# A state-space layer and a gated feed-forward: scans joined over both halves of a column, with states and decays in SBUF

## What is computed

```python
def first(x):                       # applied to layernorm(x); the result is added to x
    x, z = split(x_in @ W_in)       # 256 and 256 columns
    proj = x @ W_x                  # 256 of delta, 16 of B, 16 of C
    delta = softplus(proj[..., :256] @ W_dt + b_dt)
    dA  = exp(delta[..., None] * -exp(A_log))          # (b, l, d, n)
    dBx = (delta * x)[..., None] * B[:, :, None, :]
    def step(h, inp):
        dA_t, dBx_t, C_t = inp
        h = dA_t * h + dBx_t                            # a state for each d and n
        return h, einsum('bdn,bn->bd', h, C_t)
    y = scan(step, 0, ...) + x * D_param
    y = y * silu(z) @ W_out
    return layernorm(y + x_in) * ln_g + ln_b

def second(x):                      # applied to layernorm(x); the result is added to x
    x_prev = x shifted by one token
    r = sigmoid((mu_r*x + (1-mu_r)*x_prev) @ W_r.T)
    k = (mu_k*x + (1-mu_k)*x_prev) @ W_k.T
    return r * (square(relu(k)) @ W_v.T)
```

## Time and profile before

| | |
|---|---|
| median of 3 runs | 942.68 us (942.14 to 942.72) |
| the profiled execution | 944.42 us, its span 942.6 us |
| instructions | 15838 |
| mean granted TensorE clock | 0.973 |
| DVE | 900.9 us busy, 96% |
| POOL | 889.1 us, 94% |
| PE | 864.2 us, 92%; weight loads 688.7 us |
| ACT | 847.9 us, 90% |
| DMA | 163.60 MB, mean 174 GB/s |

### The profile page before, as it was taken

The page is one execution under the profiler, slowest core; times in us unless marked ns, Lnnn a source line. Parts: engine busy times, 40 slices in busy tenths (PEclk is TensorE's granted clock), DMA queues, the critical chain, the costliest instruction groups (busy, mean ns, idle before and its releaser), DMA issues.

```text
span 942.6 us, 15838 instructions
## 1 busy us (share of the span) xinstructions
PE 864.2 (92%) x5024; PEld 688.7 (73%) x5024; DVE 900.9 (96%) x985; ACT 847.9 (90%) x2064; POOL 889.1 (94%) x399
## 2 busy tenths in 40 slices
PE   8757679999999899989999899998999999999998
PEld 5545567877878587787868678786778768778876
DVE  4899989999999999999999999999999999999896
ACT  5886988989999999998999999999999999978875
POOL 4999999999999999999999989999999999999970
PEclk9987898999999999999999999999999999999999
DMA  7445435462534644455463644446354354446231
GB/s 222 156 177 204 175 138 204 179 235 104 210 157 161 239 164 172 183 178 166 174 248 147 224 148 160 179 179 248 125 210 179 143 198 179 157 160 223 91 101 45
DMA packets 49938, 163.60 MB, mean 174 GB/s; under 512 B 5248, under 2 KB 33152, under 8 KB 33600
## 3 DMA queue, kind: packets, MB, share of 16 engines
q1 hardware_dynamic: 48528, 161.27, 46.2%
q0 software_dynamic: 512, 1.31, 0.5%
q10 hardware_dynamic: 816, 0.02, 0.1%
HBM read 153.15 MB, written 9.44 MB: 172 GB/s over the span
## 4 chain that ended last, share of the span: by engine, by line
PE 46%; ACT 28%; DVE 15%; issue 9%; DMA 1%; POOL 0%; POOLq 0%; DVEq 0%; SPq 0%; ACTq 0%
PE w_ps L1326 10%; ACT da_ps L654 10%; PE y_ps L1317 9%; PE w_ps L1350 6%; DVE da_ps L1033 5%; PE w_ps L1359 4%; PE w_ps L1362 4%; DVE hg L1049 3%; DVE hg L1033 3%; PE w_ps L1465 3%; DVE hg L1040 2%; PE w_ps L1368 2%; ACT xn_tok L591 2%; ACT h_tok L591 2%; ACT zs L715 2%
## 5 line engine op out<-in xcount | busy, mean ns | idle before, releaser
L542 POOL TENSOR_TENSOR dbx<-u,b_ring 128x1024 f32<-128x1024 f32 x255 | 599.4, 2380 | 4.7 <-DVE hg L1033 4.6
L654 ACT ACTIVATE da_ps<-delta,a_neg 128x512 f32<-128x512 f32 x512 | 340.0, 684 | 23.9 <-DVE hg L1040 7.3
L555 POOL TENSOR_TENSOR hg<-hg,c_ring 128x1024 f32<-128x1024 f32 x122 | 290.4, 2381 | 8.5 <-ACT carry L660 6.7
L1317 PE MATMUL y_ps<-ident,hg 128*128 128x128 f32 x2048 | 264.3, 279 | 9.2 <-POOL hg L555 9.0
L1317 PEld LDWEIGHTS y_ps<-ident,hg 128*128 128x128 f32 x2048 | 241.7, 145 | 35.9 <-issue 17.8
L1033 DVE TENSOR_TENSOR_SCAN da_ps<-da_ps,carry,dbx 128x512 f32<-128x512 f32 x203 | 249.8, 1271 | 4.3 <-ACT da_ps L654 4.1
L1033 DVE TENSOR_TENSOR_SCAN hg<-da_ps,carry,dbx 128x512 f32<-128x512 f32 x181 | 220.3, 1263 | 1.4 <-ACT carry L660 1.2
L1040 DVE TENSOR_TENSOR hg<-da_ps,c_ring 128x1024 f32<-128x1024 f32 x68 | 82.3, 1210 | 0.2
L1049 DVE TENSOR_TENSOR hg<-da_ps,c_ring 128x512 f32<-128x512 f32 x130 | 82.3, 673 | 0.0
L1033 DVE TENSOR_TENSOR_SCAN da_ps<-da_ps,dbx 128x512 f32<-128x512 f32 x64 | 75.8, 1213 | 3.3 <-ACT da_ps L654 2.8
L1326 PE MATMUL w_ps<-xnT_ring,w_in 128*128 128x512 f32 x120 | 61.4, 636 | 16.0 <-ACT xT L696 14.1
(11 more groups left out here) (212 smaller groups left out, 1333.0 us busy)
## 6 DMA issues: line engine op xcount, KB each, us to landing
c_ring<-bc_rows_dram SPq DMA_DIRECT2D x64, 1024.0 KB, 4.7
b_ring<-bc_rows_dram SPq DMA_DIRECT2D x63, 1024.0 KB, 6.7
xres<-in_L_attn_x_in_dram SPq DMA_DIRECT2D x16, 512.0 KB, 4.8
x_tok<-in_L_attn_x_in_dram SPq DMA_DIRECT2D x15, 512.0 KB, 5.9
out_dram<-r_out SPq DMA_DIRECT2D x14, 512.0 KB, 3.2
bc_rows_dram<-bc_rows SPq DMA_DIRECT2D x64, 16.0 KB, 5.4
w_in<-in_L_attn_W_in_dram SPq DMA_DIRECT2D x2, 256.0 KB, 4.3
x_tok<-in_L_attn_x_in_dram SPq DMA_DIRECT2D x2, 256.0 KB, 4.6
```

Source lines behind the costliest of these rows:

```text
L542: pool.tensor_tensor(dbx[:, n % X_RING, :, :], u[:, ip, :, :], b.to_broadcast([P, KH, LC]), ALU.mult).then_inc(s["dbx_done"], 1)
L555: pool.tensor_tensor(part, part, c_of(n).to_broadcast([P, KH, LC]), ALU.mult).then_inc(s["g_pool"], 1)
L654: act.activation(da_of(n, h), delta[:, ip, h, :], ACT.Exp, scale=a_neg[:, h, n:n + 1]).then_inc(s["da_ready"], 1)
L1317: last = pe.matmul(y_tok[:, b, h * P:(h + 1) * P], hg[:, n % H_RING, h, b * P:(b + 1) * P], ident[:, :], is_transpose=True, start=n == 0 a ...
```

## The change

**One scan for a column.** `decay`, `dbx`, `u` and `hg` get rows of 515 cells (`EXT`) for each half: two lead cells, 512 tokens (`TOK`), and one cell behind. The two halves lie behind one another, so one scan of 1030 elements does both. The first cell of each half has decay 0, which ends the half before; the second has decay 1. The lead cells of `u` are 1, 0 in the first half and 0, 1 in the second; the lead cells of a B row are the two carries of that column. So POOL's product of `u` and B puts each half's carry into its lead cells, and the scan begins from there without a scalar operand. The cell behind has decay 1 and input 0: it keeps the last state where the multiplication by C, which covers only the tokens, doesn't reach it.

**Carries.** ACT copies the carries of four columns at once out of `hg` (`keep_carries`, place `KEEP_AT`) and feeds them, four columns at once, into the lead cells of the B rows (`feed_carries`, place `FEED_AT`). POOL's product waits for the feed (`carry_fed`); DVE's first scan of a group waits until the carries that its slots held are saved.

**Places in memory.** The decays are in SBUF, `decay`, a ring of three columns; the states of every column go to `hg` in SBUF, and DVE's multiplication by C works there, always in one instruction for both halves. The three PSUM banks of `da_ps` become work banks: `W_BANKS` is 6. `spare` is gone, `xn_tok` and `h_tok` serve in its place.

**Columns and places.** DVE multiplies 10 columns of a step by C in place of 8 or 9, POOL 6 in place of 7 or 8. The turn tables and `BANK` are new; of them two lines stand in the diff.

```diff
-SPLITS = [[0, 2, 5, 6, 8, 11, 12, 14], [0, 2, 3, 5, 6, 8, 11, 12, 14]]
+SPLITS = [[0, 2, 3, 5, 8, 9, 11, 12, 13, 15], [0, 2, 3, 5, 6, 9, 11, 12, 13, 15]]
-                sum1=15, sq1=16, x0=18, tanh=19, ln_exp=20, rs1=22, x1=22, sq20=22, sq21=23, rs2=23, k1=24, square=24,
+                sum1=16, sq1=17, x0=18, tanh=20, ln_exp=22, rs1=20, x1=25, sq20=23, sq21=23, rs2=23, k1=24, square=25,
-W_BANKS = 3
+W_BANKS = 6
+KEEP_AT, FEED_AT = 10, 10
-DA_BANKS = 3
+A_RING = 3
+LEAD = KH
+EXT = LEAD + LC + 1
+TOK = slice(LEAD, LEAD + LC)
...
-        u = sb("u", P, 2, KH, LC)
+        u = sb("u", P, 2, KH, EXT)
+        decay = sb("decay", P, A_RING, KH, EXT)
-        b_ring = sb("b_ring", P, BG, GN, LC)
+        b_ring = sb("b_ring", P, BG, GN, EXT)
-        dbx = sb("dbx", P, X_RING, KH, LC)
-        hg = sb("hg", P, H_RING, KH, LC)
+        dbx = sb("dbx", P, X_RING, KH, EXT)
+        hg = sb("hg", P, H_RING, KH, EXT)
...
-                sp.dma_start(b_ring[:, g % BG, :, :],
+                sp.dma_start(b_ring[:, g % BG, :, TOK],
                              bc_dram[i, GN * g:GN * g + GN, :].partition_broadcast(P)).then_inc(b_loaded[g], 16)
...
+                need(pool, s["carry_fed"], GROUPS * i + n // GN + 1)
...
-                pool.tensor_tensor(dbx[:, n % X_RING, :, :], u[:, ip, :, :], b.to_broadcast([P, KH, LC]),
+                pool.tensor_tensor(dbx[:, n % X_RING, :, :], u[:, ip, :, :], b.to_broadcast([P, KH, EXT]),
                                    ALU.mult).then_inc(s["dbx_done"], 1)
...
-                act.activation(da_of(n, h), delta[:, ip, h, :], ACT.Exp,
-                               scale=a_neg[:, h, n:n + 1]).then_inc(s["da_ready"], 1)
+                need(act, s["scan_done"], NS * i + n - A_RING + 1)
+                act.activation(decay_of(i, n)[:, h, TOK], delta[:, ip, h, :], ACT.Exp,
+                               scale=a_neg[:, h, n:n + 1]).then_inc(s["da_ready"], 1)
...
+            def keep_carries(t, g):
+                need(act, s["scan_done"], NS * t + GN * (g + 1))
+                slot = GN * g % H_RING
+                act.activation(carry[:, GN * g:GN * (g + 1), :], hg[:, slot:slot + GN, :, EXT - 1],
+                               ACT.Copy).then_inc(s["carry_saved"], 1)
+
+            def feed_carries(t, g):
+                need(act, s["dbx_done"], NS * t + GN * (g - BG + 1))
...
+                src = no_carry[:, :, :] if first else carry[:, GN * g:GN * (g + 1), :]
+                act.activation(b_ring[:, g % BG, :, 0:LEAD], src, ACT.Copy).then_inc(s["carry_fed"], 1)
...
-                for h in range(KH):
-                    in_bank = n in split_of(t) or t == LAST and n == NS - 1 and h == 1
-                    out = da_of(n, h) if in_bank else hg[:, n % H_RING, h, :]
-                    dve.tensor_tensor_scan(out, da_of(n, h), dbx[:, n % X_RING, h, :],
-                                           0.0 if first else carry[:, n, h:h + 1], ALU.mult, ALU.add).then_inc(s["scan_done"], 1)
+                if n % GN == 0:
+                    before = t if n >= H_RING else t - 1
+                    if before >= 0 and not ends(before):
+                        dve.wait_ge(s["carry_saved"], kept_groups(before) + (n - H_RING) // GN % GROUPS + 1)
...
+                dve.tensor_tensor_scan(flat(hg[:, slot, :, :]), flat(decay_of(t, n)), flat(dbx[:, at, :, :]),
+                                       0.0, ALU.mult, ALU.add).then_inc(s["scan_done"], 1)
...
-                dve.tensor_tensor(hg[:, n % H_RING, :, :], da_both(n), c_of(n).to_broadcast([P, KH, LC]),
+                part = hg[:, n % H_RING, :, TOK]
+                dve.tensor_tensor(part, part, c_of(n).to_broadcast([P, KH, LC]),
                                   ALU.mult).then_inc(s["g_vec"], 1)
```

More of the change, by code:

```diff
@@ L76, in ends @@
     return (i + 1) % CPB == 0
[L79 to L87, removed]
 def need(eng, sem, count):
@@ L193, in mamba_rwkv_layer @@
         y_tok = y_ps[:, :, :].rearrange("p a (b d) -> p (a b) d", d=D)
-        da_ps = ps("da_ps", P, DA_BANKS, LC)
         work = [ps(f"w{b}_ps", P, LC) for b in range(W_BANKS)]
-        START_BANKS = ([y_ps[:, m, :] for m in range(KH)] + [work[W_BANKS - 1][:, :]]
-                       + [da_ps[:, m, :] for m in range(DA_BANKS)])
+        START_BANKS = ([y_ps[:, m, :] for m in range(KH)] + [w[:, :] for w in work[HEAD_BANK:]])
         names = """w_in_loaded w_x_loaded w_dt_loaded w_bc_loaded w_z_loaded w_z_halved a_loaded w_loaded mu_loaded w_r_in w_kv_in ffn_turned ffn_set ident0 ident_done flags_done
@@ L323, in by_half @@
             return b[:, :].rearrange("p (k n) -> p k n", k=KH)
-        GT_LAST = K_LAST = [da_ps[:, v, :] for v in range(2)]
-        WO_LAST = R_LAST = [da_ps[:, 2, :], work[0][:, :]]
+        GT_LAST = K_LAST = [work[W_BANKS - 3 + v][:, :] for v in range(2)]
+        WO_LAST = R_LAST = [work[W_BANKS - 1][:, :], work[0][:, :]]
         HT_LAST = [y_ps[:, v, :] for v in range(2)]
@@ new lines, in scans @@
+                if t == n == 0:
+                    dve.wait_ge(s["flags_done"], FLAGS)
+                need(dve, s["y_added"], NS * t + n - H_RING + 1)
+                if n % GN == 0:
+                    before = t if n >= H_RING else t - 1
+                    if before >= 0 and not ends(before):
+                        dve.wait_ge(s["carry_saved"], kept_groups(before) + (n - H_RING) // GN % GROUPS + 1)
+                if t == n == 0 or t == LAST and n == NS - 1:
+                    for h in range(KH):
+                        if t == 0:
+                            dve.wait_ge(s["dbx_done" if h else "dbx_begun"], 1)
+                        else:
+                            need(dve, s["dbx_done"], NS * t + n + 1)
+                        need(dve, s["da_ready"], KH * (NS * t + n) + h + 1)
+                        dve.tensor_tensor_scan(hg[:, slot, h, :], decay_of(t, n)[:, h, :], dbx[:, at, h, :],
+                                               0.0, ALU.mult, ALU.add).then_inc(s["scan_done" if h else "half_scanned"], 1)
+                    return
@@ L1553, in late_v @@
                     by_token(V_LATE[v], v, kact, w_vT).then_inc(late_v_done, 1)
-                pe.wait_ge(s["scan_done"], KH * (NS * NT - 1))
-                need(pe, s["g_vec"], splits(LAST, NS - 1))
+                for b in range(W_BANKS - 3, W_BANKS):
+                    pe.wait_ge(work_read[b], sum(len(units_of(v, b)) for v in range(NT)))
                 residual(0)
```

226 lines of the change are left out of this document (98 added, 128 removed).

## The result

The changed kernel takes 1500.93 us (median of 4 runs, 1500.21 to 1503.3), the kernel before 942.7 us beside it: a ratio of 1.593, 95% interval 1.590 to 1.596. The profiled execution has a span of 1499.2 us.

A forecast was written before the change was run, and what follows sets the result against it. DVE and POOL, both full side by side, were taken to bound the kernel; taking turns, DVE's 563 + 176 and POOL's 591 + 228 add to 1558 us, with 52 at the ends 1610 us; range 1310 to 1735.

The forecast's parts named there:

- The step that decided: DVE scans and C products reading two SBUF tensors take turns with POOL products by the instruction, so times add; chance 0.78.
- The one collision from before: Kernel before, from 20.69 us: a DVE SBUF-to-SBUF `xn_tok<-x_tok` stood still 952 ns until POOL's first product ended.
- the lower end of this case: Turns by the instruction with each fixed part hidden in the wait: elements alone add to 1513 us, span 1565.
- rival B: Turns by the element: half of a scan's time stays open to POOL, 274 us less, 1336 us; chance 0.06.
- the term for POOL in the sum: 255 B products and 99 C products at full spacing, 591 + 228 us, added to DVE's time; elements only, 573 + 221.
- DVE's other groups: Six DVE groups with a PSUM operand, 125 us, can run beside POOL; up to 60 us extra only in the upper bound.
- DVE's own parts: Without turns: 254 scans of 2289 ns and 156 C products of 1216 ns, by spacing 563 us with half scans, and 176.
- ACT, the table loads, the feeds and the B rows: ACT's 27 us loss hides behind the turns; feed waits and B rows loaded as four pieces are taken at nothing.
- TensorE's granted clock: It can fall towards the lower 1.2 GHz level; even doubled work of 106 us makes a step only 8 us longer.
- Rival A: No turns between DVE and POOL: about 928 us if DVE sets the end, about 950 if ACT does; chance 0.14.
- rival C: The change doesn't do what it says, for lack of new B rows or banks: about 1000 to 1060 us; chance 0.02.
- The signs that I named: Step near 98 us, scan or `dbx` maxima about 4.6 us, PSUM groups at 0.67, DVE and POOL near 90%, ACT 55%.

The follow-up runs named there:

- experiment 1: Small kernel without the layer, DVE and POOL instructions alone and paired: ten SBUF scans took 22.06 us alone, 40.94 beside ten POOL products.
- experiment 3: Kernel before with DVE operands read from constant SBUF: products by C 1191.64 us, scans 1485.28, both 1646.82.
- experiment 4: Changed kernel with the tables of before: 1509.83 us; also scan decays from PSUM after step 0: 1121.20; also C products' states from PSUM: 1006.85.
- experiment 2: Second small kernel varying sizes and kinds of instruction: ten DVE scans took 31.24 us beside POOL products of 512, 29.19 beside POOL scalings, 22.06 alone.
- both_sbuf: Kernel before with both the scans' decay and the C products' state operand read from a constant SBUF tensor: 1646.82 us, ratio 1.745.

## Why the prediction was right, and where its size was off

The step that decided held: DVE and POOL take turns when DVE reads two SBUF tensors, by the instruction. The one collision from before, 952 ns, was of the same kind, with one SBUF tensor as in the copy of experiment 1. By the Trainium skill's page "SBUF — State Buffer", section "Who interferes with whom", the second input of DVE comes through the interface that GpSimd reads by; experiments 1, 3 and 4 agree, scans included, and its sentence that a GpSimd instruction that only writes is no obstacle to two inputs agrees with the scan beside memsets (22.06 us both ways). The prediction left out a condition of that section, by which one SBUF input is free of turns only outside what the page calls 2-port perf modes; the copy, with one SBUF input and at 0.61 us twice as fast as a product of its size (1.14), did lose 1.93 us for each POOL product. The section also says that whoever issues first has the shared ports for the whole instruction; here the measurement decides: DVE lost 1.93 us of a product's 2.30, and 0.71 of a scaling's 2.74.

The size was 7% off: 1610 forecast, 1501 measured. That is inside the stated range, but below the 1565 that I had set as the lower end of this case; it is inside only because the range reached down to 1310 for rival B, which is wrong, and that is luck. The step that failed is the term for POOL in the sum, "POOL 255 x 2.318 + 99 x 2.306 = 591 + 228", and its lower bound 573 + 221. I had let a POOL product hold the turn as long as it lasts. It costs DVE 1.93 us (experiments 1 and 2), and in this kernel DVE pays 1.62, 575 us in all: 244 us less than the 819 of the sum. Between 1.93 and 1.62 lie 108 us. That some products run beside DVE's groups with a PSUM operand would be enough for it, by an estimate: those six groups have 123 us, room for 53 products of 2.30 us, or 103 us of waits saved. But `both_sbuf` has the same groups and pays 1.90, so this part is argued and not shown. Against it I had counted DVE's other groups at nothing, "can run beside POOL"; but DVE was hardly ever idle, so they lie on its path with some 105 us by spacing. The two errors cancel in part. 1610 - 244 + 105 = 1471. The rest is 28 us: 8 in which DVE stood idle between its first scan and POOL's last product, and 20 that lie between counting the waits from durations (575) and from spacing (1499 - 52 - 8 - 563 - 176 - 105 = 595).

DVE's own parts, 254 scans of 2289 ns and products of 1216, are borne out by the shortest records, 2270 and 1192 ns. That ACT, the table loads, the feeds and the B rows cost nothing held, for the reason given: ACT stands at 59%. The B rows' landing rose from 6.7 to 7.1 us. TensorE's granted clock fell, as feared, to a mean of 0.819 from 0.973; TensorE was 66% busy, so the lower clock had room, though no run shows it by itself. (Its matmuls are 5024 in both kernels, not the 3928 of the prediction.) Rival A, no turns, is ruled out by experiments 1 and 3, and its time for that case was 20 to 40 us too low, since DVE's waits for exponentials grew (experiment 4, with the tables of before). Rival B, turns by the element, falls by 4.1 us a pair. Of rival C nothing is seen: POOL's B products waited for DVE alone (186.5 us), for no feed and no B row. The signs that I named came: scans and products with maxima of 4.5 and 4.4 us, `u<-w_ps` and `zs<-zs,w_ps` at 0.67. But POOL's share is 84% and not near 90%, with 192 us of real waiting for scans, ACT's 59% and not 55%, and the step is 90 us, (1499 - 52) / 16, not 98.

## What to carry to other kernels

Before moving an operand of VectorE from PSUM to SBUF, see whether GpSimd works beside it: with two SBUF tensors, every GpSimd product of 1024 elements that it meets costs VectorE up to 1.9 us, more than its own product of that size (1.13 us), and a busy share of 98% doesn't show it. Read the names behind the arrow and the shortest, median and longest of a line. And where two engines take turns, the account that fitted here is one engine's own time plus a price for each instruction of the other (1.62 and 1.90 us in two of these kernels); moving work to the "full" engine can then be a gain.
